# Fused Flamingo layer in f32: products with a common term share a PSUM bank, squares move to ScalarE, the down phase's sums and turnings are placed anew

## The reference

```python
# per batch of 128 tokens, D = 512
q = rms_norm(layernorm(x) @ q_w.T + q_b, norm_q_w)      # 16 heads of 32
k = rms_norm(ctx @ k_img_w.T + k_img_b, norm_k_img_w);  v = ctx @ v_img_w.T + v_img_b
x = x + tanh(g_xattn) * (attention(q, k, v) @ o_w.T + o_b)
h = layernorm(x)
r = sum of the two largest entries of h @ gate_w         # 8 experts' logits
y = square(relu(h @ up_w)) @ down_w + (h @ expert_weight) * r   # 512 -> 2048 -> 512
out = x + tanh(g_ffn) * (layernorm(y) * ln_gamma + ln_beta)
```

## Time and profile before

| | |
|---|---|
| median of 3 runs | 1590.77 us (1587.71 to 1596.41) |
| the profiled execution's own time | 1587.87 us |
| its span | 1586.1 us |
| PE busy / matmuls | 1319.6 us (83%) / 9154 |
| DVE busy / instructions | 1064.7 us (67%) / 1512 |
| ACT busy / instructions | 639.2 us (40%) / 1888 |
| POOL busy / instructions | 969.0 us (61%) / 977 |
| mean DMA rate | 183 GB/s |
| chain that ended last | PE 37%, POOL 24%, DVE 12%, issue 9%, DMA 7%, SPq 4%, ACT 3% |

### The profile page before, as it was taken

How to read it: one execution, slowest core, us unless ns; L and a number is a source line. 1 busy time by engine, 2 the same in 40 slices (tenths; PEclk the granted TensorE clock), 3 DMA queues, 4 the chain that set the end, 5 groups by cost and what they waited for, 6 DMA issues and landing times.

```text
span 1586.1 us, 26472 instructions
## 1 busy us (share of the span) xinstructions
PE 1319.6 (83%) x9154; PEld 1111.3 (70%) x9154; DVE 1064.7 (67%) x1512; ACT 639.2 (40%) x1888; POOL 969.0 (61%) x977
## 2 busy tenths in 40 slices
PE   7989999999998999779789485879847877989991
PEld 5867777777777777569678365767636866867981
DVE  6776666766687667557768275675645776665795
ACT  6866666766676752124321003431000433112430
POOL 4766666666589648763946464592456476455394
PEclk9998999999999999899999787999869899999996
DMA  6688888888787456677556655546656554555731
GB/s 214 143 226 222 222 205 206 219 207 206 193 201 186 107 173 206 213 180 244 179 167 209 158 164 151 206 154 207 196 136 155 195 171 156 192 191 167 214 106 53
DMA packets 388452, 289.55 MB, mean 183 GB/s; under 512 B 283771, under 2 KB 298235, under 8 KB 383230
## 3 DMA queue, kind: packets, MB, share of 16 engines
q1 hardware_dynamic: 350856, 178.90, 43.0%
q10 hardware_dynamic: 37494, 109.33, 20.4%
HBM read 205.08 MB, written 83.10 MB: 182 GB/s over the span
## 4 chain that ended last, share of the span: by engine, by line
PE 37%; POOL 24%; DVE 12%; issue 9%; DMA 7%; SPq 4%; ACT 3%; ACTq 0%; DVEq 0%; POOLq 0%
PE wide L79 11%; PE wide L80 10%; PE wide L81 10%; DMA pair<-x_scratch 5%; POOL hid L2084 5%; DVE wo_lo L1911 4%; PE wide L418 3%; SPq L1604 2%; PE wide L406 2%; PE wide L427 2%; POOL fxy L2088 2%; POOL hid L2073 2%; DMA out_x<-fxy 1%; POOL pair L2106 1%; POOL hid L2075 1%
## 5 line engine op out<-in xcount | busy, mean ns | idle before, releaser
L1911 DVE TENSOR_TENSOR wo_lo<-hid,wo_hi 128x512 fp32r<-128x512 f32 x224 | 262.3, 1208 | 142.1 <-ACT wo_hi L1771 141.9
L79 PE MATMUL wide<-eight,wo_hi 128*128 128x256 f32 x512 | 152.7, 298 | 63.7 <-DVE wo_lo L1911 55.0
L817 ACT ACTIVATE prob<-wide,nmx 128x128 f32<-128x128 f32 x512 | 182.2, 408 | 35.5 <-DVE nmx L628 35.5
L988 POOL TENSOR_TENSOR prob<-prob,rr 128x512 f32<-128x512 f32 x128 | 132.7, 1049 | 104.3 <-DVE rr L636 102.9
L2084 POOL TENSOR_TENSOR hid<-hid 128x512 f32<-128x512 f32 x96 | 157.8, 1669 | 56.4 <-DVE wo_lo L1911 56.4
L1771 ACT ACTIVATE hid<-wide 128x512 f32<-128x512 f32 x64 | 38.1, 598 | 360.9 <-PE wide L81 360.9
L1771 ACT ACTIVATE wo_hi<-hid 128x512 fp32r<-128x512 f32 x224 | 135.4, 625 | 112.9 <-PE wide L81 112.9
L79 PEld LDWEIGHTS wide<-eight,wo_hi 128*128 128x128 f32 x512 | 99.9, 195 | 74.9 <-issue 48.0
L80 PE MATMUL wide<-eight,wo_hi 128*128 128x256 f32 x512 | 146.8, 287 | 0.0
L81 PE MATMUL wide<-eight,wo_lo 128*128 128x256 f32 x512 | 146.5, 286 | 0.0
L817 ACT ACTIVATION_READ_ACCUMULATOR prob<-wide,nmx 128x1 f32 x512 | 127.4, 249 | 0.0
(11 more groups left out here) (276 smaller groups left out, 4214.6 us busy)
## 6 DMA issues: line engine op xcount, KB each, us to landing
eight<-down_scratch ACTq DMA_DIRECT2D x32, 1024.0 KB, 5.8
xn_scratch<-xs SPq DMA_DIRECT2D x48, 256.0 KB, 5.1
wk_hi<-down_scratch ACTq DMA_DIRECT2D x12, 1024.0 KB, 5.4
wk_lo<-down_scratch ACTq DMA_DIRECT2D x12, 1024.0 KB, 6.1
hid<-xn_scratch SPq DMA_DIRECT2D x48, 256.0 KB, 3.2
wk_hi<-up_scratch ACTq DMA_DIRECT2D x12, 1024.0 KB, 4.8
eight<-up_scratch ACTq DMA_DIRECT2D x12, 1024.0 KB, 7.0
wk_lo<-up_scratch ACTq DMA_DIRECT2D x12, 768.0 KB, 5.7
```

What stands on the lines that cost most here:

```text
L79: eng.matmul(dst, ah, bh, start=first and k == 0, stop=False)
L817: i = act.activation(prob[par][:, g, h * P:(h + 1) * P], cols(bank[g], h), ACT.Exp, bias=nmx[:, n:n + 1], scale=1.0, accum_out=rs[:, n:n + 1])
L988: pool.tensor_tensor(p, p, r, ALU.mult).then_inc(po_p, 1)
L1911: dve.tensor_tensor(ff.s_lo[k % KT], hid[q][:, ff.D_SEQ[m][1], :], ff.s_hi[k % KT].bitcast(F32), ALU.subtract).then_inc(ff.dv_l, 1)
```

## The change

1. `mm3` takes `onto`: a product may go on in a bank that another product has filled. In the up phase products 6, 7 and 4 go on in the bank of product 1 (bank "A") and product 3 in that of product 5 ("B"), each after ACT or DVE has read what stood there; product 2 has bank "C". A and B alternate between two banks by q. Order on PE: 1, 5, then product 4 of q-1, then 6, 2, 3, 7.
2. `sum_2`, `sum_3` (as it was), `finish`, the squares on DVE (L1896), POOL's `middle` and `s1` go. In their place ACT makes three copies, a Relu of 128x512 out of PSUM (`relu_21`), a Relu of 128x1024 and a Square of 128x1536 (`squares`); DVE makes `add_11`, `add_22`, `add_12`, one square of 128x512 and a new `sum_3`.
3. The operands S2 and S1 of the down phase are made on DVE while PE does the experts (`sums_21`, 16 additions), S4 in the down phase on DVE (`sum_4`, 8 additions at k = 18 to 25). POOL's `s234` and `add_V` and ACT's `copy_V` go.
4. In the down phase the order of products is `D_SEQ = (0, 3, 4, 2, 5, 1, 6)`; m = 2, 3, 4 and 6 go on in the banks of m - 2. Each product has one `collect` of 128x1024 on DVE: 7 in all.
5. The 16 turnings of the next group stand at k = 9 to 52; ACT's `hi_T` comes two steps behind DVE's transpose. POOL's 16 `lo_T` are all that POOL has in a down phase of groups 0 to 2.
6. SP's deals, x loads, result stores and residual loads stand at other parts q, x statistics of the second half at q = 5 (was 6); y rows are taken in natural order.
7. In the attention phase DVE's `unit_lo_sums` is cut in two single subtractions, behind the V bias and one reciprocal, where both stood ahead of the maxima.
8. The order of products and turnings at the passage from attention to group 0 is written anew.

The core of the diff:

```diff
                         ff.stats(dve, 0, ff_pair(s) + GB)
-                    if ff.second_of(s, par) is not None:
-                        ff.unit_lo_sums(dve, ff.second_of(s, par))
                     maxima(s, 0)
                     maxima(s, 1)
                     maxima(s, 2)
@@ -744,7 +740,11 @@
                     maxima(s, 3)
                     inverse(s, 0)
                     bias_v(n, 1 - par)
+                    if ff.second_of(s, par) is not None:
+                        ff.unit_lo_sums(dve, ff.second_of(s, par), 0)
                     inverse(s, 1)
+                    if ff.second_of(s, par) is not None:
+                        ff.unit_lo_sums(dve, ff.second_of(s, par), 1)
                     if dealt(n + 1):
                         turn_x(n + 1)
                     inverse(s, 2)
@@ -1115,22 +1115,28 @@
     tb = (at("tb_hi", [P, KT, D], early + 2 * KB8, F32R), at("tb_lo", [P, KT, D], early + 3 * KB8, F32R))
```

```diff
+
+    KINDS = ("xa", "ta", "xb", "tb")
     XOP = {"xa": xa, "ta": ta, "tb": tb, "xb": xb}
     NT = KT * len(KINDS)
     T_BANK = (6, 7, 5, 0, 6, 5, 7, 2, 6, 7, 1, 2, 0, 3, 2, 0)
     XS_AT = {"xa": 0, "xb": 2, "ta": 4, "tb": 6}
 
-    U_SEQ = ((0, 0, xa, 0), (0, 1, xa, 2), (0, 3, ta, 2), (0, 2, ta, 0), (1, 1, tb, 0), (1, 0, tb, 2), (1, 2, xb, 2))
-    U_BANK = (4, 5, 6, 7, 1, 0, 2)
-
-    D_SEQ = ((3, 1), (0, 0), (4, 1), (6, 3), (1, 2), (5, 3), (2, 2))
+    PRODUCT = {1: (0, 0, xa, 0), 2: (0, 1, xa, 2), 3: (1, 2, xb, 2), 4: (1, 0, tb, 2), 5: (0, 2, ta, 0), 6: (0, 3, ta, 2), 7: (1, 1, tb, 0)}
+    A_BANK, B_BANK, C_BANK = (4, 7), (5, 0), 6
+    E_BANK = (1, 2, 0, 5, 4, 6, 7, 5)
+    U_ORDER = [(0, p) for p in (1, 5, 2, 6, 3, 7)]
+    for u in range(1, NQ):
+        U_ORDER += [(u, 1), (u, 5), (u - 1, 4), (u, 6), (u, 2), (u, 3), (u, 7)]
+    U_ORDER.append((NQ - 1, 4))
+
+    D_SEQ = (0, 3, 4, 2, 5, 1, 6)
```

```diff
+    def product(pe, g, q, p):
+        which, op, (x_hi, x_lo), kk = PRODUCT[p]
         w = chunk_slot(2 * q + which)
         low = (3 if which else 4) * H
         stat = [tuple(w[:, at0 + op * H + k * P:at0 + op * H + (k + 1) * P] for at0 in (0, low)) for k in range(2)]
-        mm3(pe, bank[U_BANK[n]], stat, [(x_hi[:, kk + k, :], x_lo[:, kk + k, :]) for k in range(2)]).then_inc(pe_P, 1)
-
...
+    def upward(pe, g, q, p):
+        n = g * NQ + q
+        if p in (1, 3):
+            chunk_ready(pe, g, 2 * q + (p == 3))
+        if g == 0 and q == 0 and p != 4:
+            pe.wait_ge(dv_T, {1: 4, 5: 8, 2: 9, 6: 9, 3: 12, 7: 16}[p])
+        elif g > 0 and q == 0 and p in (1, 5, 3, 7):
+            pe.wait_ge(po_lT, (g - 1) * NT + {1: 4, 5: 8, 3: 12, 7: 16}[p])
+        if p == 1:
+            if q > 1:
+                pe.wait_ge(ac_21, n - 1)
+            elif g > 0:
+                pe.wait_ge(dv_D, NC * g - 1)
+        if p == 5:
+            if q > 1:
+                pe.wait_ge(dv_U, 3 * (n - 2) + 2)
+            elif g > 0 and q == 1:
+                pe.wait_ge(dv_D, NC * g)
+        if p == 2 and q > 0:
+            pe.wait_ge(dv_U, 3 * (n - 1) + 1)
+        if p in (6, 3, 7):
+            pe.wait_ge(ac_P, 3 * n + {6: 1, 3: 2, 7: 3}[p])
+        if p == 4:
+            pe.wait_ge(dv_U, 3 * n + 3)
+        product(pe, g, q, p)
```

```diff
                 if g > 0:
-                    for i in {2: (0,), 3: (1,), 4: (2, 3), 5: (4,), 7: (5,)}.get(q, ()):
+                    for i in {2: (0, 1), 4: (2, 3), 6: (4,)}.get(q, ()):
                         store_out(g - 1, i)
                         load_res(g - 1, i + 2)
                 if more:
@@ -1662,14 +1688,16 @@
                     if q == 3:
                         deal_t(g + 1, 0)
                         load_x(g + 1, 1)
+                    if q == 6:
+                        deal_x(g + 1, 1)
                     if q == 7:
-                        deal_x(g + 1, 1)
-            if more:
-                deal_t(g + 1, 1)
+                        deal_t(g + 1, 1)
             if g == 0:
                 ff.piece_store(sp, NQ)
                 ff.piece_store(sp, NQ + 1)
             else:
+                store_out(g - 1, 5)
+                load_res(g - 1, 7)
                 store_out(g - 1, 6)
                 store_out(g - 1, 7)
             if more:
```

```diff
+        def copy_a6(g, q):
+            act.wait_ge(ff.pe_P, ff.produced(g, q, 6))
+            copy(hid[q][:, 1, :], bank[ff.A_BANK[q % 2]]).then_inc(ff.ac_P, 1)
+
+        def relu_21(g, q):
+            act.wait_ge(ff.pe_P, ff.produced(g, q, 4))
+            act.activation(hid[q][:, 2, :], bank[ff.A_BANK[q % 2]], ACT.Relu).then_inc(ff.ac_21, 1)
+
+        def squares(g, q):
             n = g * NQ + q
-            act.wait_ge(ff.pe_P, NC * n + 4)
-            copy(hid[q][:, 3, :], bank[ff.U_BANK[3]]).then_inc(ff.ac_P, 1)
+            act.wait_ge(ff.dv_U, 3 * n + 2)
+            h = hid[q][:, 0:2, :]
+            act.activation(h, h, ACT.Relu).then_inc(ff.ac_sq, 1)
+            act.wait_ge(ff.ac_sq, 2 * n + 1)
+            act.wait_ge(ff.ac_21, n + 1)
+            h = hid[q][:, 0:3, :]
+            act.activation(h, h, ACT.Square).then_inc(ff.ac_sq, 1)
```

```diff
+            n = g * NQ + q
+            dve.wait_ge(ff.dv_U, 3 * n + 3)
+            h = hid[q][:, 3, :]
+            dve.scalar_tensor_tensor(out=h, in0=h, scalar=0.0, in1=h, op0=ALU.max, op1=ALU.mult).then_inc(ff.dv_22, 1)
 
         def sum_3(g, q):
+            dve.wait_ge(ff.ac_sq, 2 * (g * NQ + q + 1))
+            dve.tensor_tensor(hid[q][:, 1, :], hid[q][:, 0, :], hid[q][:, 1, :], ALU.subtract).then_inc(ff.dv_3, 1)
+
+        def sums_21(g, q):
             n = g * NQ + q
-            dve.wait_ge(ff.pe_P, NC * n + 5)
-            dve.wait_ge(ff.dv_U, 5 * n + 1)
-            dve.tensor_tensor(hid[q][:, 2, :], bank[ff.U_BANK[4]], hid[q][:, 1, :], ALU.add).then_inc(ff.dv_U, 1)
-
-        def finish(g, q):
-            n = g * NQ + q
-            dve.wait_ge(ff.pe_P, NC * n + 7)
-            dve.wait_ge(ff.po_U, 2 * n + 1)
-            dve.tensor_tensor(hid[q][:, 1, :], bank[ff.U_BANK[6]], hid[q][:, 1, :], ALU.add).then_inc(ff.dv_U, 1)
-            dve.wait_ge(ff.po_U, 2 * n + 2)
-            dve.tensor_tensor(hid[q][:, 2, :], hid[q][:, 2, :], bank[ff.U_BANK[5]], ALU.subtract).then_inc(ff.dv_U, 1)
-            for m in range(2):
-                dve.wait_ge(ff.dv_U, 5 * n + 4 + m)
-                h = hid[q][:, 2 * m:2 * m + 2, :]
-                dve.scalar_tensor_tensor(out=h, in0=h, scalar=0.0, in1=h, op0=ALU.max, op1=ALU.mult).then_inc(ff.dv_h, 1)
+            if q == 0:
+                dve.wait_ge(ff.pe_P, NK * (g + 1))
+            dve.wait_ge(ff.dv_22, n + 1)
+            dve.wait_ge(ff.dv_3, n + 1)
+            dve.tensor_tensor(ff.S24[:, q, :], hid[q][:, 3, :], hid[q][:, 1, :], ALU.subtract).then_inc(ff.dv_12, 1)
+            dve.wait_ge(ff.dv_12, 2 * n + 1)
+            dve.tensor_tensor(ff.S1[:, q, :], ff.S24[:, q, :], hid[q][:, 0, :], ALU.add).then_inc(ff.dv_12, 1)
+
+        def sum_4(g, q):
+            dve.wait_ge(ff.dv_l, NK * g + 2 * NQ + q + 1)
+            dve.tensor_tensor(ff.S24[:, q, :], hid[q][:, 2, :], ff.S24[:, q, :], ALU.subtract).then_inc(ff.dv_4, 1)
...
+        def collect(g, m):
+            a, b = ((0, 0), (1, 1), (0, 1), (0, 1), (1, 1), (0, 0), (1, 0))[m]
+            dst = quadrant[a][b]
             dve.wait_ge(ff.pe_S, NK * g + NQ * (m + 1))
-            dve.tensor_tensor(dst, dst, partial(m), op).then_inc(ff.dv_D, 1)
-
```

```diff
-                    x_stats(g + 1, 0)
-                if q == 2:
-                    x_normal(g + 1, 0)
-                if q == 6:
-                    x_stats(g + 1, 1)
-                if q == 7:
-                    x_normal(g + 1, 1)
+            if g > 0:
+                for i in {4: (2, 3)}.get(q, ()):
+                    result(g - 1, i)
+                for i in {0: (0, 1), 3: (2, 3), 4: (4,), 7: (5, 6)}.get(q, ()):
+                    y_centre(g - 1, i)
+            if g < LAST:
+                if q in (1, 5):
+                    x_stats(g + 1, q // 5)
+                if q in (2, 6):
+                    x_normal(g + 1, q // 6)
```

549 lines of the change are left out of this document (236 added, 313 removed).

## The result

The changed kernel takes **1452.53 us** (median of 4 runs, 1449.91 to 1458.65) against 1591.36 us before (median of 4 runs): 0.913 of the time, 95% interval 0.909 to 0.917. The prediction said 1434 us, in a range of 1378 to 1478. The direction and the range held; the gain of 139 us is 16 us less than the -155 us of the sum. The execution that was profiled is the slowest of the four: 1458.65 us, span 1456.9, 129 us less than the profiled one of before.

The account below looks back on a forecast made before the run. Each phase had its own limit: PE waited on DVE's low parts in attention, on DVE stretched by POOL in down phases, on SP's deals in groups 1 and 2. Terms summed to -155 us, giving 1434 us, range 1378 to 1478.

Parts of the forecast that it names:

- Part 2: Down phases: DVE relieved of POOL's stretching, PE sets the pace at 85 us; -22, -23, -24, -9 us by group.
- The factor 0.39: Down phases: us by which DVE's low parts are stretched per us of POOL work; 9 us of stretching forecast.
- Part 1: Attention: unit low parts behind the maxima, 56.5 us gross, partly given back by late deals of x; -22 us.
- rival B: Attention: the burst takes everything back, PE's clock falling behind late deals; +22, 1456 us; chance 0.17.
- Part 3: Group 0 up and experts: POOL loses work, a little less than half of PE's 20.5 us idle goes; -9 us.
- Part 4: Groups 1 and 2 up and experts: first stall goes, new 22 us stall at q = 5, last shrinks; -17 and -20 us.
- to 5 or 6: Groups 1 and 2: the last stall, 16 us before, shrinks to 5 or 6 because second deals come 11 us earlier.
- Rival A: Groups 1 and 2: deals not in the way, no stall at q = 5; -42 more, 1392 us; chance 0.2.
- Part 5: Group 3 up and experts: no deals, chains through POOL gone, 113.3 to 104 us; -9 us.
- Part 6: Up phase, accumulating in one bank: ACT's copy has over 2 us of cover between products; no term in the sum.
- rival D: Up phase: the chain PE, copy, PE stalls PE in each of 32 parts; 1590 us or more; chance 0.02.
- Rival C: Down phases: DVE stays the limit, low parts meeting POOL's in lumps; 90 us per phase, 1454 us; chance 0.12.

Follow-up runs that it names:

- c: Changed kernel with the feed-forward deals written in rows of 2 KB instead of 128 bytes (output not the layer's): 1407.01 us, one run.
- k: Changed kernel with small transfers ahead of deals, POOL's x work first, experts' load earlier, attention's high-part stores and next load earlier: 1402.96 us (median of 6).
- l: Changed kernel with experts' second load earlier, y stores ahead of the last four deals, attention's high-part stores and next load earlier: 1409.22 us (median of 6).
- b: Changed kernel with 24 more POOL additions of 128x512 in each down phase of groups 0 to 2: 1471.19 us, one run.
- f: Changed kernel with the last four deals of a group issued behind y stores 5 to 7: 1447.62 us, one run.

## Why the prediction was right, and where not

*Part 2, the down phases* (-78 predicted, -93 measured): the mechanism came as forecast. DVE was stretched by POOL, POOL was relieved, DVE fell to 60.9 us and PE's pace, 80.8 us, became the limit. The extra POOL work brought 8 us of 28 back, so its share in the whole gain is shown in part. Mis-sized was one term: 5.4 us for starts and changes of product, taken from group 3. In fact PE goes from one product to the next without any pause, and PE's idle time in group 3 before was waiting for DVE too. The factor 0.39 measured 0.45. DVE was busy 61 us where 72 were forecast (63 of its own and 9 of stretching): 56 x (0.76 - 0.68), some 5 us, was all the stretching there was, with POOL's 16 low parts spread over the phase; four low parts and one collect fall outside the phase's edges, and the records of neighbouring DVE instructions overlap by 4 us.

*Part 1, attention* (-22 predicted): -10 in the two traces, -12 to -18 against the six other traces of the same attention phase, 12 by undoing it. The named cause is right, burst over the deal of x, and so is the size of its delay (the deal 3.7 us late, forecast 3.3). The failed step is "if all of that reaches PE, 2.3 us per unit are left": 2.4 to 2.7 us of the delay reached PE as waiting, but the slower clock behind the wait, which the text kept for the lower bound only, cost some 2 us more (slots of 19.4 and 19.7 us instead of 15.1), and by undoing it 1.2 us per unit are left instead of 2.3. By the medians rival B, which gives everything back, lies about as near as the forecast.

*Part 3, group 0* (-9 predicted, 0 measured): the step that failed is "a little less than half of the idle time". POOL's busy time fell from 96.5 to 57.6 us and its waits grew by as much:

```profile
629.36 0.74 POOL L1324 TENSOR_TENSOR sums<-fxy 128x256 f32<-128x256 f32 x1 [7.94 <-DMA fxy<-in_up]
...
646.45 0.72 POOL L1324 TENSOR_TENSOR pair<-fxy 128x256 f32<-128x256 f32 x1 [11.79 <-DMA fxy<-in_up]
```

The chain was loads of raw pieces, behind stores and deals in SP's queue. The two edits that lighten or reorder that queue gave 5 us (c) and 7 us (k against l), where the phase differs by up to 4 us among traces of kernels that leave it alone. So this chain is read from the trace, and that it is all that holds group 0 is not shown.

*Part 4, groups 1 and 2* (-17 and -20 predicted, -9 and -16 measured, -9 to -12 and -14 to -18 over the traces that leave them alone): the stall at q = 5 came where it was put, by the chain that was given, with 15.6 us (12.35, and 3.2 for the part before) instead of 22, because eight deals took 33.8 us and not 42. The failed step is the end: "to 5 or 6". Measured there are 10.2 us for the y stores and 5.45 us for the experts' second load. That load is late by the change itself: its slot of the ring is read by product 4, and product 4 of a part now runs as the third product of the next part, so ACT may issue the load only then. No step of the prediction asked when a ring slot comes free. And PE's busy time, held at 108 us, measured 112.5: with it group 1 adds up, 112.5 + 15.6 + 5.45 + 10.2 = 143.7; what makes it longer is open. Rival A (deals not in the way) is refuted: taking their rows away was worth 43 us, the price that it was given (42), but they are in the way. (In its working, eight deals at 1.3 us end 32 us earlier and not 26; nothing in it hangs on that.)

*Part 5, group 3* (-9 predicted, -0.8 measured): the failed step is that nothing new would hold PE. The same load was overlooked: 3.25 us of waiting for it, 2.4 for a y store, and a clock of 0.60 in the 7.3 us behind the wait took what the shorter chains gave. The clock was the larger term and partly bad luck: with the same wait and no fall behind it (b and f) the phase takes 110 us, with the load earlier 109.5. Even then it stays 5 us above the forecast 104.

*Part 6* held: PE waits once for one of ACT's copies between two products of a bank, 1.27 us at the start of group 0, and never after, so rival D has no place. Rival C (lumps) did not come with 16 low parts on POOL, but it came at once with 24 additions more. The Trainium skill's rule weighed beside it ("SBUF — State Buffer", Who interferes with whom) has a second half that the runs bear out: with POOL at 62 instead of 22 us the low parts, two inputs in SBUF, went from 0.79 to 1.28 us, while the collects, one input in PSUM, stayed at 1.21 and the transposes, one input, at 0.70. What it says of the size, an exclusive lock, the trace bears out as well, instruction by instruction: every low part that began inside one of POOL's operations in run b ended 0.54 to 0.58 us after it. The prediction's reading, that 0.39 us per us is less than a full lock, and its 87 us for DVE under one, are both wrong: it added POOL's whole busy time to DVE's, but only the operation that comes second pays, and only the rest of the first one's time.

That the total came within 1.3% owes something to errors of both signs: 15 us too little in the down phases, 40 too much elsewhere, in the profiled execution. (By its own sum, 1433 for the profiled execution and 2.9 for the median, the forecast should have read 1436.)

## What to carry to other kernels

When a wait is removed, ask of every transfer that was issued behind it what it will now lie over, and of every buffer whose reader was moved when its next load may start; the first took back most of what attention had to give, and the second, with the slower clock behind its wait, what group 3 had; both cost groups 1 and 2 a part. A store that needs only half of its data can go when that half is ready, and the next load ahead of the other half: the two together were worth 33 us here in one run (29 to 38 us of the attention phase), more than the reordering on DVE that they repaired. And where two engines wait in one queue's shadow, the trace names the later one; removing it alone (the x loads) gained nothing.

## What the runs showed of the hardware that was not expected

- A wait of PE of 2.4 to 2.7 us cost 4.3 to 4.6 us in all. The stretches behind the 2.41 us wait in attention and behind the 3.25 us one in group 3 show a granted clock of 0.68 and 0.60: part of each at the lower of the two levels, 1.2 GHz, after PE had stood idle. The fall is not certain: behind waits of 3.31 and 3.23 us for the same load, in runs b and f, the granted clock was 1.00, and their group 3 is 4 us shorter for it.

```profile
314.70:320.00 5.30, 5.26 (x20) 4.31 (x21) 3.36 (x7) 1.43 (x4) 3.03 (x4) 0.68 0.81 182
...
1312.70:1320.00 7.30, 7.30 (x20) 5.79 (x21) 2.69 (x5) 0.86 (x2) 1.34 (x2) 0.60 0.26 69
```

- A deal of 256 KB in rows of 128 bytes took SP between 1.3 us (four in 5.33) and 8.0 us (four in 31.98), the latter beside ring loads of 1 MB, with no change in itself. In rows of 2 KB it took 1.6 us.
- Two subtractions on the same shapes differ by a factor of 1.9 in time (0.68 to 1.28 us in the mean) by what POOL does beside them. One that begins inside a POOL operation ends 0.54 to 0.59 us after it, in group 1's down phase before, after and in run b, but for one that began at the same moment as POOL's and was not held.
